# Attention with all four score tiles of a head pair in one group, small row jobs between V and Q in the bank of z, and one reciprocal and one value scaling per pair

## The chip, the cores and the metric

The kernel runs on one core of one Trainium2 chip. The core has TensorE (PE, matrix products into PSUM), VectorE (DVE), ScalarE (ACT), GpSimd (POOL), and SyncE (SP), which only issues transfers. PSUM is eight banks of 128 x 512 fp32 numbers. The metric is the device time of the whole program in microseconds (us).

## The reference

Four layers follow each other on x of 8 rows (batch entries) x 512 positions x 128 features: softmax attention with 16 heads, a mixture of experts, linear attention with an MLP, and the same mixture of experts again. The change touches the first layer, and one bank name in what follows it:

```python
def _L0_attn_a_ref(x, W_K, W_Q, W_V, W_O):      # 16 heads of 64
    k = jnp.einsum('ahe,bce->bach', W_K, x)
    q = jnp.einsum('ahe,bce->bach', W_Q, x)
    v = jnp.einsum('ahe,bce->bach', W_V, x)
    scores = jnp.einsum('bach,baCh->bacC', k, q)
    mask = jnp.tril(jnp.ones((seq, seq), dtype=scores.dtype))
    masked = jnp.tril(scores) - 10000000000.0 * (1.0 - mask)
    attn = jax.nn.softmax(masked / np.sqrt(d_head), axis=-1)
    z = jnp.einsum('bach,bacC->baCh', v, attn)
    z_flat = z.transpose(0, 2, 1, 3).reshape(b, seq, -1)
    return jnp.einsum('ef,bcf->bce', W_O, z_flat)
...
x = x + _L0_attn_a_ref(_layernorm(x, axis=-1), ...)
x = x + _L0_ffn_ref(_layernorm(x, axis=-1), ...)
```

The softmax runs over the axis C, up to the position c of the key side, so each of the 512 positions c has a row of scores of length c + 1. The sum over each row divides V, not the scores.

## The kernel before

**Tiling.** The order on every engine is written out by hand, and each engine runs its own list; semaphores tie them together. The attention stage goes over 8 rows b, in each over 8 head pairs g (`PAIRS`). The two heads of a pair lie in partitions 0 to 63 and 64 to 127. Positions c are cut into four tiles i of 128, and tile i has `width[i]` = 128, 256, 384, 512 columns of scores, since the mask cuts the rest. A pair was handled in two halves n = 2g and 2g + 1 (`HALVES`): the even half takes the "big" tile 3 and the "small" tile 0, the odd half takes tile 2 and tile 1.

**Work of a pair on TensorE.** `scores(b, n)` (L1159) makes the scores of a half: three products (high and low parts of K and Q) for each of the two heads. After the even half come V for a later pair (`project_V`, into `bankK`), Q for pair g + 1 (`project_Q`, into `bankQ`), the output product of an older pair (`out_of`, L1189, which needs the high and low part of its z), and K for pair g + 1 (`project_K`, into `bankK`). These projections all go through `matmul3` (L451 to L453). After the odd half comes `PV` (L1176) of the pair g - 1: probabilities times scaled V, summed over tiles in `bankZ`.

**The other engines.** VectorE adds the mask to each score tile and takes its negated maximum in one instruction (L1449, eight in a pair: four tiles x two heads), makes the low parts of Q, K and z (`low_Q` L1411, `low_K` L1416, `low_z` L1421), and inverts the sums of a half (`invert`, L1426). ScalarE takes the exponentials with their sums (L1350) and copies V, Q, K and z out of PSUM (L1329, L1318, L1322, L1335). GpSimd scales V by the inverted sums (`scale_V`, L1526), once in a half.

**Small row jobs.** Beside the pairs, each row b has jobs for its neighbours: the statistics, the norm and the transposes for the next row (`ahead`), the transposes that bring the output of the row before back (`turn_back`, L1199), and for the row before the router of the experts: transposes (L426), logits (L547), choice of two experts, ranks (L624 to L628), slots, and eight scatters from GpSimd (L675). Constants such as `TURN_AT = 5` name the half in which each stands. All TensorE jobs of this kind use `bankQ`, stand behind the `PV` of an odd half, and `project_Q` of the next pair waits for their readers. A semaphore tells how far each step is; `START` is its first value. `each_row` (L459) writes the eight rows one after another.

**After the rows**, the last pairs are finished, and `Folding` prepares weights of later layers; it uses banks 2 and 3 as `bankVO`.

## Time and profile before

| what | us |
|---|---|
| runs of the kernel, median (lowest to highest) of 3 | 1360.21 (1359.12 to 1361.42) |
| span of the profiled execution | 1361.0 |
| attention pairs, first score product to first score product of the last pair | 18.15 to 527.66 |
| PE busy in the span | 1219.8 (90%) |
| DVE, ACT, POOL busy in the span | 920.1, 824.2, 517.2 |

The page tells how long each engine was busy and where in the span. A busy engine need not be at its peak, so the step from the start of one instruction to the start of the next is what counts on TensorE. The profiled execution lies within the three runs, 0.8 us above their median. The views used further down are the busy time of each engine in a stretch, the timeline of one engine or of all (start, duration, what it is, and in brackets the idle time in front of it with what ended it), and the same busy time for VectorE alone.

### The profile page before, as it was taken

Reading aid. Unit: us, or ns where it says so; the run is one execution under the profiler, and the core shown is the slowest. Engines: PE = TensorE matmul, PEld = TensorE weight load, DVE = VectorE, ACT = ScalarE, POOL = GpSimd, SP = SyncE. Lnnn points to the kernel's source line nnn. Section 1 sums busy time; section 2 is a strip of 40 time slices with the busy share of each in tenths; the row PEclk is TensorE's granted clock in tenths of the full one; section 3 lists DMA queues with packets and bytes.
Section 4 is the critical chain, followed back from the end, with each engine's and each line's share of the span. In section 5 each row is a group of like instructions: output and inputs, shape, how many; then the busy total and the mean of one; then the engine's idle time right before and its main releaser. Section 6 shows DMA issues by size and latency. Waiting matters only on the chain. (4 is left out here: it accounts for less than half of the span.)

```text
span 1361.0 us, 27110 instructions
## 1 busy us (share of the span) xinstructions
PE 1219.8 (90%) x7787; PEld 924.5 (68%) x7787; DVE 920.1 (68%) x3602; ACT 824.2 (61%) x2478; POOL 517.2 (38%) x683
## 2 busy tenths in 40 slices
PE   6999999999999998599993999999996998199990
PEld 5666666666666665499982777777774665199890
DVE  6777888888888876444445788888874666244445
ACT  5888888888888886144441556555655675044440
POOL 2112332323333232545452343344433376545450
PEclk9999999999999999799996999999998999599995
DMA  9100000000000000222222000000000011222225
GB/s 295 42 1 1 9 9 9 10 9 10 9 10 9 10 13 5 68 63 70 70 67 66 17 17 16 17 1 1 1 1 1 15 40 36 73 64 71 68 71 193
DMA packets 54445, 52.92 MB, mean 39 GB/s; under 512 B 7341, under 2 KB 43098, under 8 KB 54330
## 3 DMA queue, kind: packets, MB, share of 16 engines
q1 hardware_dynamic: 36320, 29.39, 7.6%
q0 software_dynamic: 8928, 17.84, 3.9%
q10 hardware_dynamic: 9082, 4.33, 1.1%
q8 instruction: 52, 0.85, 0.3%
q14 instruction: 63, 0.52, 0.1%
HBM read 29.48 MB, written 22.05 MB: 38 GB/s over the span
## 5 line engine op out<-in xcount | busy, mean ns | idle before, releaser
L1350 ACT ACTIVATE prob<-prob,negmax 128x512 f32<-128x512 f32 (+3 forms) x512 | 283.0, 556 | 78.8 <-DVE negmax L1449 76.8
L1449 DVE CUSTOM_DVE_ANT_0 prob<-bank,mask 128x512 f32<-128x512 f32 (+3 forms) x512 | 227.7, 482 | 51.2 <-PE bank L1159 50.9
L1526 POOL TENSOR_TENSOR Vs<-Vh_sb,rinv 128x256 f32<-128x256 f32 x128 | 78.4, 612 | 364.6 <-DVE rinv L1426 364.4
L1047 POOL DMA_INDIRECT expert_out<-f_x_yb,f_x_to x142 | 136.5, 961 | 155.3 <-DVE f_x_yb L1035 100.5
L1176 PE MATMUL bank<-prob,Vs 128*64 128x512 f32 (+3 forms) x1024 | 151.9, 439 | 0.9 <-DVE zT_lo L1421 0.9
L675 POOL DMA_INDIRECT expert_in<-f_xn,f_slot x128 | 126.9, 991 | 51.2 <-issue 27.9
L979 PE MATMUL bank<-f_x_xbT,W_sb 128*128 128x256 f32 x568 | 138.5, 388 | 1.5 <-DVE f_x_xbT L1015 1.5
L1000 ACT ACTIVATE f_x_hid<-bank,cols 128x256 f32<-128x256 f32 x144 | 63.6, 475 | 93.0 <-PE bank L979 93.0
L979 PEld LDWEIGHTS bank<-f_x_xbT,W_sb 128*128 128x128 f32 x568 | 104.6, 194 | 14.7 <-DVE f_x_xbT L1015 2.9
L1176 PEld LDWEIGHTS bank<-prob,Vs 128*64 128x64 f32 x1024 | 63.4, 136 | 69.5 <-issue 59.4
L1000 ACT ACTIVATE prob<-bank,cols 128x256 f32<-128x256 f32 x140 | 61.1, 475 | 81.7 <-PE bank L979 81.7
L1032 DVE CAST f_x_to<-f_x_this_to 128x1 int32<-128x1 f32 x142 | 21.4, 151 | 115.0 <-DMA expert_out<-f_x_yb,f_x_to 114.4
L1350 ACT ACTIVATION_READ_ACCUMULATOR prob<-prob,negmax 128x1 f32 x512 | 97.3, 190 | 0.0
L1159 PE MATMUL bank<-Q_hi,K_hi 64*128 64x512 f32 (+3 forms) x512 | 93.3, 357 | 2.7 <-DVE K_lo L1416 2.1
L1809 ACT ACTIVATE yT_hi<-bank 128x512 fp32r<-128x512 f32 x64 | 38.3, 598 | 92.7 <-PE bank L1736 92.7
L1943 DVE SCALAR_TENSOR_TENSOR z_sb<-bank,ro,z_sb 128x128 f32<-128x128 f32 x256 | 88.5, 346 | 5.0 <-POOL ro L1877 1.5
L1159 PE MATMUL bank<-Q_lo,K_hi 64*128 64x512 f32 (+3 forms) x512 | 83.5, 318 | 0.0
L1159 PE MATMUL bank<-Q_hi,K_lo 64*128 64x512 f32 (+3 forms) x512 | 83.5, 318 | 0.0
L1159 PEld LDWEIGHTS bank<-Q_hi,K_hi 64*128 64x128 f32 x512 | 48.5, 183 | 44.4 <-issue 34.6
L1816 ACT ACTIVATE junk<-bank 128x128 f32<-128x128 f32 x256 | 68.7, 274 | 15.5 <-PE bank L453 3.4
L451 PE MATMUL bank<-WVO_hi,yT_hi 128*128 128x256 f32 x256 | 73.9, 289 | 2.4 <-DVE z_sb L1943 2.4
L453 PE MATMUL bank<-WVO_hi,yT_lo 128*128 128x256 f32 x256 | 71.5, 279 | 0.0
(263 smaller groups left out, 3183.6 us busy)
## 6 DMA issues: line engine op xcount, KB each, us to landing
f_x_xb<-expert_in SPq DMA_DIRECT2D x73, 130.0 KB
b_crows<-expert_out SPq DMA_DIRECT2D x16, 256.0 KB, 2.8
c_crows<-expert_out SPq DMA_DIRECT2D x16, 256.0 KB, 4.1
expert_out<-f_x_yb,f_x_to POOLq DMA_INDIRECT x142
expert_in<-fill ACTq DMA_DIRECT2D x16, 130.0 KB, 2.6
x_sb<-in_L_attn_a_x_dram SPq DMA_DIRECT2D x8, 256.0 KB, 6.2
W_sb<-in_L_ffn_W_dram SPq DMA_DIRECT2D x1, 2048.0 KB, 9.9
expert_in<-f_xn,f_slot POOLq DMA_INDIRECT x128
```

The source lines that it names most:

```text
L451: nc.tensor.matmul(ps, lhsT_hi, rhs_hi, start=True, stop=False)
L453: return nc.tensor.matmul(ps, lhsT_lo, rhs_hi, start=False, stop=stop)
L675: pool.indirect_dma_start(xg, bass.IndirectOffsetOnAxis(ap=self.slot[:, u, t, k:k + 1], axis=0), self.norm.xn_sb[:, u, t, :], None).then_i ...
L979: nc.tensor.matmul(self.bankH[c][:, 0:BLK], W1_sb[:, e, c * P:(c + 1) * P], self.xbT[:, :], start=True, stop=True).then_inc(self.up_done[c ...
L1000: nc.scalar.activation(self.hid[:, c, :], self.bankH[c][:, 0:BLK], ACT.Relu, bias=b1_col[:, e * FC + c:e * FC + c + 1]).then_inc(self.hid_ ...
L1047: pool.indirect_dma_start(yg, bass.IndirectOffsetOnAxis(ap=self.to[:, t:t + 1], axis=0), self.yb[:, t, :], None).then_inc(self.stored[t], 16)
L1159: mm = nc.tensor.matmul(bankS[which][a][:, 0:width[i]], left[r, g % 2, tile], right[r, g % 2, 0:width[i]], start=(right is Q_hi and left i ...
L1176: mm = nc.tensor.matmul(bankZ[heads, 0:width[tiles_of(m)[which]]], Vs[:, m % 4, AT[which], heads], prob[:, m % 4, a, columns_of(m, which)] ...
L1350: nc.scalar.activation(mine, mine, ACT.Exp, scale=-1.0, bias=negmax[:, n % 4, t, a:a + 1], accum_out=rowsum[:, n % 4, t, a:a + 1]).then_in ...
L1449: nc.vector.tensor_tensor_reduce(out=prob[:, n % 4, a, columns_of(n, which)], in0=bankS[which][a][:, 0:width[i]], in1=mask[:, T - width[i] ...
L1526: nc.gpsimd.tensor_tensor(Vs[:, m % 4, :, :].rearrange("p t (a d) -> p t a d", a=2), V_sb[:, quarter % 2, small:big + 1:big - small, pair] ...
L1943: nc.vector.scalar_tensor_tensor(out=tile, in0=bankO[s % 2 * 2 + m // 2][:, o:o + D], scalar=ro[:, s % 2, m:m + 1], in1=tile, op0=ALU.mult ...
```

## The change

1. **Scores.** `scores(b, g)` makes all four tiles of a pair in one group, in the order 1, 3, 0, 2. Tile 1 goes into `bankQ` and `bankK`, tile 3 into the big banks, tiles 2 and 0 share the small banks (tile 0 behind the columns of tile 2). One wait for the masks of the pair before stands ahead of the group; V waits until the two masks of tile 1 are done.
2. **Order on TensorE.** A pair is now: scores, V, small row job (`between`), Q, `out_of` of pair g - 2 (before: g - 3), K, `PV` of pair g - 1. `between` waits in each pair until `low_z` of pair g - 2 is done, whether a job follows or not. The jobs write `bankZ`; `between_read` makes `PV` wait for their readers.
3. **VectorE.** The eight masks of a pair stand in a row; behind the second comes the reciprocal of all eight sums of pair g - 1, behind the third `low_z`, behind the sixth the readers of a row job; then `low_Q`, `low_K`, and only then the other row work of the pair.
4. **ScalarE.** It begins a pair with z of pair g - 2, then eight exponentials, with V behind the third, Q behind the fourth and K behind the sixth.
5. **GpSimd.** One `scale_V` per pair over 512 numbers a partition in place of two over 256; up to two scatters stand together in a pair.
6. `prob`, `Vs`, `negmax`, `rowsum` and `rinv` are laid out in two buffers by pair in place of four by half; `Folding` uses banks 0 and 3.

```diff
-            ahead = Ahead("a", st, LN, x_sb, 1.0, None, split=True, whole=False, bankT=bankQ)
+            ahead = Ahead("a", st, LN, x_sb, 1.0, None, split=True, whole=False, bankT=bankZ)
...
-            TURN_AT = 5
-            AHEAD_STATS, AHEAD_RSTD, AHEAD_NORM, AHEAD_TR = 0, 1, 2, 3
-            X_ADD, ROUTE_STATS, ROUTE_RSTD, ROUTE_NORM, ROUTE_TR, ROUTE_LOGITS, ROUTE_RANK = 5, 6, 7, 8, 9, 11, 15
+            AHEAD_STATS, AHEAD_RSTD, AHEAD_NORM, AHEAD_TR = 0, 1, 1, 3
+            TURN_AT, ROUTE_STATS, ROUTE_RSTD, ROUTE_NORM, ROUTE_TR, ROUTE_LOGITS, ROUTE_RANK = 2, 2, 3, 3, 4, 5, 7
...
+            SCATTERS = {0: (0, 1), 1: (2,), 2: (3, 4), 3: (5,), 4: (6, 7)}
+
+            ORDER = [(i, a) for i in (1, 3, 0, 2) for a in range(2)]
...
+                    def scores(b, g):
+                        pe.wait_ge(masked, START + (b * PAIRS + g) * PER_PAIR)
+                        pe.wait_ge(q_ready, START + b * PAIRS + g + 1)
+                        pe.wait_ge(k_ready, START + b * PAIRS + g + 1)
+                        for i in (1, 3, 0, 2):
...
+                    def between(b, u, g, first, last):
...
+                        pe.wait_ge(zT_ready, START + b * PAIRS + g - 1)
+                        if g == TURN_AT and not first:
+                            turn_back(b - 1)
+                        if g == AHEAD_TR and not last:
+                            ahead.pe_transpose(pe, b + 1, 1 - u)
...
+                        for g in range(PAIRS):
+                            scores(b, g)
...
+                                pe.wait_ge(masked, START + (b * PAIRS + g) * PER_PAIR + 2)
                                 project_V(u if quarter < NT else 1 - u, quarter % NT, part)
...
+                            between(b, u, g, first, last)
+                            if ahead_too:
                                 project_Q(*here)
-                                if g >= 3:
-                                    out_of(b, g - 3)
+                            if g >= 2:
+                                out_of(b, g - 2)
...
                                 project_K(*here)
...
+                            between_read(b, g, first, last)
...
                             if g >= 1:
-                                PV(b, n - 3)
-                                PV(b, n - 2)
+                                PV(b, g - 1)
...
-                    invert(B - 1, HALVES - 1)
                     low_z(B - 1, PAIRS - 2)
+                    invert(B - 1, PAIRS - 1)
                     low_z(B - 1, PAIRS - 1)
```

**TensorE, second half of a pair, before** (a_xnT with WVO is K for the next pair, Q with K are scores, prob with Vs is `PV`; L1199 is the row job `turn_back`):

```order
L451 MATMUL bank<-a_xnT_hi,WVO_hi 128x512
L452 MATMUL bank<-a_xnT_lo,WVO_hi 128x512
L453 MATMUL bank<-a_xnT_hi,WVO_lo 128x512
L1159 MATMUL bank<-Q_hi,K_hi 128x384 x2
L1159 MATMUL bank<-Q_lo,K_hi 128x384 x2
L1159 MATMUL bank<-Q_hi,K_lo 128x384 x2
L1159 MATMUL bank<-Q_hi,K_hi 128x256 x2
L1159 MATMUL bank<-Q_lo,K_hi 128x256 x2
L1159 MATMUL bank<-Q_hi,K_lo 128x256 x2
L1176 MATMUL bank<-prob,Vs 64x512 x2
```

**TensorE, the same place of the changed program**, from K on:

```order
L454 MATMUL bank<-a_xnT_hi,WVO_hi 128x512
L455 MATMUL bank<-a_xnT_lo,WVO_hi 128x512
L456 MATMUL bank<-a_xnT_hi,WVO_lo 128x512
L1176 MATMUL bank<-prob,Vs 64x512 x2
L1176 MATMUL bank<-prob,Vs 64x128 x2
L1176 MATMUL bank<-prob,Vs 64x256 x2
L1176 MATMUL bank<-prob,Vs 64x384 x2
L1164 MATMUL bank<-Q_hi,K_hi 128x256 x2
L1164 MATMUL bank<-Q_lo,K_hi 128x256 x2
L1164 MATMUL bank<-Q_hi,K_lo 128x256 x2
L1164 MATMUL bank<-Q_hi,K_hi 128x512 x2
```

The score group between K and `PV` is gone; `PV` follows K at once, and the scores of all tiles follow `PV`.

**VectorE, before, around the choice of experts** (halves 12 and 13 of a row; ISA is the mask instruction with its accumulator read, f_ex to f_row_sel belong to the router):

```order
L593 CAST f_topidf<-f_topid 128x32
L594 TENSOR_TENSOR gates<-f_top,f_rrec 128x8
L1449 ISA prob,negmax<-bank,mask 128x384
...
L1426 RECIPROCAL rinv<-rowsum 128x4
L1416 TENSOR_TENSOR K_lo<-bank,K_hi 128x512
L1449 ISA prob,negmax<-bank,mask 128x256
...
L600 COPY f_xn<-token 128x4
L602 COPY f_xn<-f_topidf 128x4
L604 TENSOR_TENSOR f_is_k<-expert_id,f_topidf 128x32 x2
```

**VectorE, the same router work in the changed program**, at the end of pair 6 of a row:

```order
L1411 TENSOR_TENSOR Q_lo<-bank,Q_hi 128x512
L1416 TENSOR_TENSOR K_lo<-bank,K_hi 128x512
L582 TENSOR_REDUCE f_rsum<-f_ex 128x4
L584 MAX f_top<-f_ex 128x8 x4
L589 RECIPROCAL f_rrec<-f_rsum 128x4
L591 MAX_INDEX f_topid<-f_top,f_ex 128x8 x4
L596 CAST f_topidf<-f_topid 128x32
L597 TENSOR_TENSOR gates<-f_top,f_rrec 128x8
L603 COPY f_xn<-token 128x4
L605 COPY f_xn<-f_topidf 128x4
L607 TENSOR_TENSOR f_is_k<-expert_id,f_topidf 128x32 x2
```

Masks of score tiles stood between the two parts of this work; now both parts stand together, behind `K_lo`.

## Rows read from the trace of the kernel before

**Rows 1.** Busy time of each engine in a stretch of the pairs (start:end, length):

```profile
core 0: us, PE busy (x) PEld busy (x) DVE busy (x) ACT busy (x) POOL busy (x), PEclk, DMA share, GB/s
215.00:275.00 60.00, 59.31 (x430) 40.48 (x430) 49.15 (x209) 50.58 (x154) 20.14 (x30) 1.00 0.03 11
```

**Rows 2.** Timeline of PE over one pair: start, duration, engine, line, operation:

```profile
283.86 0.50 PE L1159 MATMUL bank<-Q_hi,K_hi 64*128 64x512 f32 x2
...
285.05 0.39 PE L451 MATMUL bank<-WVO_hi,a_xnT_hi 128*128 128x256 f32 x1
...
285.87 0.40 PE L451 MATMUL bank<-a_xnT_hi,A_hi 128*128 128x512 f32 x1
...
288.04 0.44 PE L1159 MATMUL bank<-Q_hi,K_hi 64*128 64x384 f32 x2
...
289.12 2.37 PE L1176 MATMUL bank<-prob,Vs 128*64 128x512 f32 x16
...
291.43 0.66 PE L426 MATMUL bank<-ident,a_xn 128*128 128x128 f32 x4
...
292.01 0.51 PE L1159 MATMUL bank<-Q_hi,K_hi 64*128 64x512 f32 x2
```

**Rows 3.** Timeline of PE at row jobs; brackets: idle before, and its releaser:

```profile
276.09 0.19 PE L624 MATMUL bank<-f_sel,before_bf 128*128 128x32 bf16 x1
...
296.06 0.50 PE L451 MATMUL bank<-a_xnT_hi,WVO_hi 128*128 128x512 f32 x1 [0.21 <-ACT Vh_sb L1329]
...
319.24 0.50 PE L451 MATMUL bank<-a_xnT_hi,A_hi 128*128 128x512 f32 x1 [0.39 <-ACT f_xnT L433]
...
324.90 1.06 PE L547 MATMUL bank<-Wr_sb,f_xnT 128*128 128x8 f32 x8
325.89 0.50 PE L1159 MATMUL bank<-Q_hi,K_hi 64*128 64x512 f32 x2
...
341.13 0.19 PE L624 MATMUL bank<-f_sel,before_bf 128*128 128x32 bf16 x1
```

**Rows 4.** Timeline of DVE in the same pair:

```profile
285.02 0.69 DVE L1449 CUSTOM_DVE_ANT_0 prob<-bank,mask 128x512 f32<-128x512 f32 x1 [0.74 <-PE bank L1159]
...
285.64 0.69 DVE L1449 CUSTOM_DVE_ANT_0 prob<-bank,mask 128x512 f32<-128x512 f32 x1
...
286.74 0.69 DVE L1421 TENSOR_TENSOR zT_lo<-bank,zT_hi 128x512 fp32r<-128x512 f32 x1
...
290.16 0.17 DVE L1426 RECIPROCAL rinv<-rowsum 128x4 f32<-128x4 f32 x1
290.25 0.66 DVE L1416 TENSOR_TENSOR K_lo<-bank,K_hi 128x512 fp32r<-128x512 f32 x1
...
290.83 0.41 DVE L1449 CUSTOM_DVE_ANT_0 prob<-bank,mask 128x256 f32<-128x256 f32 x1
```

**Rows 5.** Timeline of ACT in the same pair:

```profile
286.48 0.58 ACT L1329 ACTIVATE Vh_sb<-bank 128x512 f32<-128x512 f32 x1
...
286.96 0.59 ACT L1318 ACTIVATE Q_hi<-bank 128x512 fp32r<-128x512 f32 x1
...
287.44 0.72 ACT L1350 ACTIVATE prob<-prob,negmax 128x512 f32<-128x512 f32 x1
...
288.14 0.40 ACT L1350 ACTIVATE prob<-prob,negmax 128x128 f32<-128x128 f32 x1
```

**Rows 6.** DVE busy in four stretches: router norm, experts' choice (two parts), statistics:

```profile
312.82:314.87 2.05, 2.05 (x9) 1.00 0.19 65
330.20:331.60 1.40, 1.33 (x17) 1.00 0.00 0
333.91:334.76 0.85, 0.78 (x8) 1.00 0.00 0
345.66:346.96 1.30, 1.16 (x9) 1.00 0.15 51
```

**Rows 7.** Timeline of all engines behind the last pair's scores:

```profile
527.66 0.50 PE L1159 MATMUL bank<-Q_hi,K_hi 64*128 64x512 f32 x2
...
535.03 0.66 DVE L1421 TENSOR_TENSOR zT_lo<-bank,zT_hi 128x512 fp32r<-128x512 f32 x1
535.25 0.61 POOL L1526 TENSOR_TENSOR Vs<-Vh_sb,rinv 128x256 f32<-128x256 f32 x1 [2.06 <-DVE rinv L1426]
535.74 0.20 PEld L1176 LDWEIGHTS bank<-prob,Vs 128*64 128x64 f32 x4 [1.37 <-DVE zT_lo L1421]
```

More of the change, by code:

```diff
@@ new lines, in between_read @@
+                    def between_read(b, g, first, last):
+                        if g == TURN_AT and not first:
+                            pe.wait_ge(x_done, START + b)
+                        if g == AHEAD_TR and not last:
+                            pe.wait_ge(xnT_ready, START + b + 2)
+                            pe.wait_ge(ahead.lo_ready, START + b + 2)
+                        if g == ROUTE_TR and not first:
+                            pe.wait_ge(route.xnT_ready, START + b)
+                        if g == ROUTE_LOGITS and not first:
+                            pe.wait_ge(route.step, START + (b - 1) * route.DVE_STEPS + route.LOGIT)
+                        if g == ROUTE_RANK and not first:
+                            pe.wait_ge(route.step, START + (b - 1) * route.DVE_STEPS + route.PLACE)
@@ L1207, in row @@
                     def row(b, u):
                         first, last = is_row(b, 0), is_row(b, B - 1)
-                        for n in range(HALVES):
-                            g = n // 2
-                            scores(b, n)
-                            if n % 2 == 0:
-                                if g == PAIRS - 1 and last:
-                                    out_of(b, g - 3)
-                                    continue
+                        for g in range(PAIRS):
+                            scores(b, g)
+                            ahead_too = g < PAIRS - 1 or not last
+                            here = (b, u, g + 1) if g < PAIRS - 1 else (b + 1, 1 - u, 0)
+                            if ahead_too:
@@ L1222, in row @@
-                                if n == AHEAD_TR + 1 and not last:
-                                    pe.wait_ge(xnT_ready, START + b + 2)
-                                    pe.wait_ge(ahead.lo_ready, START + b + 2)
-                                if n == ROUTE_TR + 1 and not first:
-                                    pe.wait_ge(route.xnT_ready, START + b)
-                                if n == ROUTE_LOGITS + 1 and not first:
-                                    pe.wait_ge(route.step, START + (b - 1) * route.DVE_STEPS + route.LOGIT)
@@ L1257, in row @@
-                            if n == ROUTE_RANK and not first:
-                                pe.wait_ge(q_ready, START + b * PAIRS + g + (1 if last else 2))
-                                route.pe_rank(pe, b - 1, 1 - u)
+                                PV(b - 1, PAIRS - 1)
                     pe.wait_ge(startup.const, startup.CONSTS)
@@ L1375, in row @@
+                            if g == TURN_AT - 1 and not first:
+                                evac_out(b - 1)
+                            if g == ROUTE_LOGITS and not first:
                                 route.act_exp(act, b - 1, 1 - u)
@@ new lines, in row @@
+                                if j == 2 and g >= 2:
+                                    low_z(b, g - 2)
+                                elif j == 2 and not first:
+                                    low_z(b - 1, PAIRS + g - 2)
+                                if j == 5:
+                                    if g == 0 and first:
+                                        startup.dve_cols(dve)
+                                        folding.dve_early(dve)
+                                    if g == TURN_AT and not first:
+                                        x_add(b - 1)
+                                    if g == AHEAD_TR and not last:
+                                        ahead.dve_low(dve, b + 1, 1 - u, xnT_ready)
+                                    if g in (ROUTE_LOGITS, ROUTE_RANK) and not first:
+                                        ROUTE_DVE[g][0](dve, b - 1, 1 - u)
@@ L1472, in row @@
+                            if g < PAIRS - 1 or not last:
+                                low_Q(*here)
+                                low_K(*here)
                             if not last:
-                                if n == AHEAD_STATS:
+                                if g == AHEAD_STATS:
                                     if first:
```

318 lines of the change are left out of this document (138 added, 180 removed).

## The prediction

> **What bounds the kernel now.** I read the busy times by stretch first. In a stretch in the middle of the pairs TensorE is busy 59.31 of 60.00 us at full clock (1.00 of 2.4 GHz), VectorE 49.15, ScalarE 50.58, GpSimd 20.14 [rows 1]. So TensorE sets the pace, and only what shortens its list, or the waits in it, brings time. Then I read TensorE's timeline as steps from start to start. A pair without a row job takes 283.86 to 291.43, 7.57 us: first score group 1.19, V 0.82, Q with `out_of` and K 2.17, second score group 1.08, `PV` 2.31 [rows 2]. A row of eight pairs takes 341.13 - 276.09 = 65.04 [rows 3], while 8 x 7.57 = 60.56. The other 4.5 us of a row are row jobs and the waits they cause: 0.58 for four transposes [rows 2], 0.99 for the logits, and waits such as 0.39 for the router's copy and 0.21 for V's [rows 3]. A product that starts after a wait or a change of tile shape lasts 0.50 in place of 0.40, so a fresh start costs 0.10 [rows 2, 3].
>
> **One score group in place of two.** The products are the same. Two groups cost 1.19 + 1.08; one group saves a fresh start (0.10) and one change of shape at its end (0.09, taken like the start: the rows don't separate it, its bounds are 0 and 0.2). It costs 2.08. TensorE alone would need 2.08 + 0.82 + 2.17 + 2.31 = 7.38 for a pair.
>
> **The new wait between V and Q.** `between` waits in every pair for `low_z`. What stands ahead of it on VectorE: the first mask, which began 1.16 behind the first score product for 512 columns [rows 2, 4]. Tile 1 has 256 columns; its three products are shorter by about 0.12 each, so the mask can begin at 0.80. Two masks of 256 columns take 0.34 each (0.41 less the 0.07 by which neighbours overlap), the reciprocal 0.09 (290.16 to 290.25), a mask of 512 columns 0.62, `low_z` 0.69 [rows 4]. That ends at 0.80 + 0.68 + 0.09 + 0.62 + 0.69 = 2.88. TensorE followed `low_z` by 0.05 where it waited for it (535.69 to 535.74) [rows 7]: Q can start at 2.93. V ends at 2.08 + 0.82 = 2.90. The two are level, and Q then pays a fresh start. A pair is 2.93 + 0.10 + 2.17 + 2.31 = 7.51, only 0.06 under 7.57. The gain of the merged group is thus nearly eaten by the wait. Queued behind this wait are Q, `out_of`, K and `PV`, and whoever needs them; every us by which VectorE comes late to its first mask is a us of TensorE.
>
> **Row jobs between V and Q.** A job now stands where TensorE starts afresh anyhow, so it costs its time less 0.10: three times transposes 0.48, logits 0.89, ranks about 0.12 (bounds 0.05 and 0.25). Sum 2.45. Their readers have Q, `out_of` and K as cover, 2.17, and the readers (a copy of 0.6 to 0.8 and a subtraction of 0.7) fit. The old waits of 0.39, 0.21 and the like go.
>
> **What is late next: VectorE's row work.** It stands behind `K_lo` now, in fewer and larger pieces. When is `K_lo` done? ScalarE begins the third exponential at 1.57 + 0.74 = 2.31; 0.70 for it, V's copy from 3.09 when V is there, 0.48; the fourth exponential 0.70 to 4.27; Q's copy 0.48; two of 128 columns 0.39 each; K's copy begins at 5.53 and lasts 0.58 [rows 5]; `K_lo` takes 0.58 more [rows 4] and ends at 6.7. The next pair wants VectorE at 7.51 + 0.80 = 8.31, so 1.6 us are free. Statistics (1.30) fit, the norm of the next row (half of the 2.05 of the router's norm) fits. The router's norm (2.05) does not: in pair 3 the copy of the transposes pushes `K_lo` to 7.27, it ends at 9.32, and pair 4, which is 7.98 behind, wants VectorE at 8.78: 0.54 late. The experts' choice (1.40 + 0.85) ends at 8.97 against 8.31: about 0.7 late [rows 6]. Together 1.24 in a row of eight pairs.
>
> **GpSimd, reciprocal, scatters.** One scaling of 512 in place of two of 256 lasts between 0.61 and 1.22 [rows 7]; I take 1.1. It starts near 1.9 of a pair, `PV` needs it at 5.1, so even with two scatters behind it nobody waits. The saved reciprocal is 0.09 of VectorE in the second half of a pair, where it is waiting for K: nothing. In the Trainium skill, GPSIMD Engine Reference, section 3.1, a two-input elementwise operation costs about 2.6 cycles per element, an estimate of 0.55 us for the 256 more, thus 1.16; no run here shows it yet. The sum below would be 0.06 higher by it, at the tail alone.
>
> **Tail.** Before, the last `PV` began 8.08 behind the first score product of the last pair [rows 7]. Now: VectorE 0.7 late, ranks at 3.6, their reader done at 4.7, `PV` of pair 6 from 4.8 to 7.2, its copy to 7.8, `low_z` to 8.5. The last reciprocal stands behind that, 8.6, scaling to 9.85, last `PV` at 9.9: 1.8 later. I take 1.9.
>
> **The sum.** A full row: 8 x 7.51 + 2.45 + 1.24 = 63.77, which is 1.27 less than 65.04; six such rows give 7.6. Rows 0 and 7 have fewer jobs; I take 2.3 for both, with half a us from the start, where the first K no longer waits behind statistics. Minus the tail: 7.6 + 2.3 - 1.9 = 8.0. Against the profiled span, 1361.0 - 8.0 = 1353.0. The median is 0.8 below that span, so 1352.2.
>
> **Rivals.**
> *TensorE keeps its own pace.* If the wait at Q is not felt, a pair is 7.38. It gives 0.13 more in the six pairs of a row that are not late, 6 us in all: 1346. For it: 2.88 and 2.90 are level. Against it: the wait has to be over 0.1 earlier for the fresh start to vanish too.
> *The chain is a tenth longer.* The first mask at 0.90 in place of 0.80 (a shape that no row shows) gives 0.8 a row, 6.4 in all: 1359, no change.
> *Slower: `K_lo` comes late.* VectorE's row work can't start before it, and ScalarE is 84% busy [rows 1]. If ScalarE delivers K so late that `K_lo` ends just when the next scores start (0.8 later than above), the two late pairs cost 0.8 more each, both statistics 0.5 each and the next row's norm 0.2: 2.8 a row, 19 over seven rows, and the time is 1364. It decides from about 0.43 later on, where it costs 1.14 a row and eats the gain. For it: three copies in one pair (V, Q, K) and row jobs on ScalarE shift K; against: I count 1.6 us of slack.
> *GpSimd blocks VectorE.* The scaling, now twice as long, lies beside the mask and `low_z` of the chain. If it held `low_z` from 2.2 to 3.0, each of 64 pairs would lose 0.8, 51 in all: 1403. Against it: `low_z` and masks beside scalings last the same 0.69 as elsewhere [rows 4, 7]. The Trainium skill, SBUF — State Buffer, section "Who interferes with whom", says that only VectorE instructions with two SBUF inputs or in a two-port mode contend with GpSimd; mask and `low_z` read one input from PSUM, so by that rule, too, this rival falls.
> *The change does less than it says.* Merged reciprocal and scaling are off the path; they give nothing in any case above.
>
> **How the numbers follow.** Chances: the forecast 0.48 (1347 to 1356, from the bounds of the shape change, the ranks and the two late pairs), TensorE's pace 0.12, longer chain 0.20, late `K_lo` 0.18, GpSimd 0.02. The range that leaves out no more than 0.2 reaches from 1344 to 1365. A measurement of this kernel can tell 0.2% (2.7 us) from no change. Faster by more than that: 0.48 + 0.12 = 0.60; within it: 0.20; slower: 0.20.
>
> **What would show it.** In the timeline after: Q starts 2.9 to 3.1 behind the first score product in pairs without a job, with a duration of 0.50; a pair takes 7.5; pairs 4 and 7 show V or Q waiting 0.5 to 0.7 for VectorE; waits of TensorE for the copies of row jobs are gone; the last `PV` is about 10 behind the last pair's first score product. It is wrong if the first masks begin later than 0.9, if `K_lo` ends later than 7.2 of a pair, or if more than two pairs of a row are late.

## The result, and the profile after

| | kernel before | changed kernel |
|---|---|---|
| median of 4 runs (lowest to highest), us | 1360.07 (1359.12 to 1361.42) | 1351.72 (1348.61 to 1353.20) |
| ratio (95% interval) | 1 | 0.9937 (0.9925 to 0.9949) |
| span of the profiled execution | 1361.0 | 1346.7 |
| first score product of the last pair | 527.66 | 516.40 |
| last `PV` | 535.74 | 526.46 |
| behind it | 825.3 | 820.2 |

The change saves 8.4 us in the medians, which ends 0.5 us below the forecast of 1352.2. A second series of the same two kernels, further down, gave a ratio of 0.9948, or 5.9 us, so that the forecast came this close to the median is partly luck.

The profiled execution is the shortest of the four; its span is 14.3 us below that of before. A time is 1.9 us longer than the span of the same execution (1348.61 against 1346.7), so the profile of the kernel before, with its span of 1361.0, stands for a time near 1362.9: 2.8 above the median of that kernel and not, as the section on the profile before says, within its runs. The two profiles thus lie further apart than the medians. 9.3 of the 14.3 us lie in the attention, up to the last `PV`. The rest lies behind it, in code that the change hardly touches (one bank name); an experiment below takes that up.

Busy time in the same 60 us as in [rows 1] (columns as there):

```profile
215.00:275.00 60.00, 58.94 (x431) 40.46 (x429) 50.12 (x209) 52.19 (x156) 19.74 (x23) 1.00 0.03 9
```

TensorE has a little more idle time than before (1.06 us against 0.69) and yet a row is 1.2 us shorter. The table of pairs below tells where: an ordinary pair gives 0.05, 0.4 in a row, and the pairs with row jobs, which cost 4.5 us a row more than ordinary ones before, now cost 3.6 more. So most of the gain comes in the pairs with row jobs, whose place is new, and less in the ordinary ones. An ordinary pair, TensorE's timeline; it answers to [rows 2]:

```profile
333.75 0.39 PE L1164 MATMUL bank<-Q_hi,K_hi 64*128 64x256 f32 x2
...
335.86 0.39 PE L454 MATMUL bank<-WVO_hi,a_xnT_hi 128*128 128x256 f32 x1
...
336.67 0.50 PE L454 MATMUL bank<-a_xnT_hi,A_hi 128*128 128x512 f32 x1
337.01 0.40 PE L455 MATMUL bank<-a_xnT_lo,A_hi 128*128 128x512 f32 x1
...
338.96 2.37 PE L1176 MATMUL bank<-prob,Vs 128*64 128x512 f32 x16
...
341.27 0.39 PE L1164 MATMUL bank<-Q_hi,K_hi 64*128 64x256 f32 x2
```

Scores 2.11, V 0.81, Q at 2.92 with its first product 0.50 long in place of 0.40, the pair 7.52. VectorE in the same pair, as [rows 4]:

```profile
334.55 0.42 DVE L1448 CUSTOM_DVE_ANT_0 prob<-bank,mask 128x256 f32<-128x256 f32 x1 [1.02 <-PE bank L1164]
...
335.25 0.20 DVE L1426 RECIPROCAL rinv<-rowsum 128x8 f32<-128x8 f32 x1
335.36 0.64 DVE L1448 CUSTOM_DVE_ANT_0 prob<-bank,mask 128x512 f32<-128x512 f32 x1
...
335.93 0.69 DVE L1421 TENSOR_TENSOR zT_lo<-bank,zT_hi 128x512 fp32r<-128x512 f32 x1
...
339.94 0.69 DVE L1416 TENSOR_TENSOR K_lo<-bank,K_hi 128x512 fp32r<-128x512 f32 x1 [0.56 <-ACT K_hi L1323]
```

The first mask begins 0.80 behind the first score product, `low_z` ends at 335.93 + 0.69 = 336.62, and Q starts 0.05 later. The late pairs are there too. In pair 4 the router's norm ends on VectorE just where the next mask starts, 1.44 behind the scores' start of 364.59 and not 0.80, and TensorE waits at the row job:

```profile
363.98 1.10 DVE L404 TENSOR_SCALAR f_xn<-x_sb,f_mv,f_power 128x128 f32<-128x128 f32 x4
365.00 1.11 DVE L410 TENSOR_SCALAR x_sb<-x_sb,f_power 128x128 f32<-128x128 f32 x4
366.03 0.42 DVE L1448 CUSTOM_DVE_ANT_0 prob<-bank,mask 128x256 f32<-128x256 f32 x1
```

```profile
368.14 0.65 PE L427 MATMUL bank<-ident,f_xn 128*128 128x128 f32 x4 [0.32 <-DVE zT_lo L1421]
```

And pair 7 of a row (scores from 325.28), where the first mask comes 1.62 behind, after the experts' choice:

```profile
326.74 0.21 DVE L619 TENSOR_REDUCE f_row_sel<-f_sel 128x8 f32<-128x32 bf16 x1
326.90 0.42 DVE L1448 CUSTOM_DVE_ANT_0 prob<-bank,mask 128x256 f32<-128x256 f32 x1
```

```profile
327.73 0.38 PE L454 MATMUL bank<-WVO_hi,a_xnT_hi 128*128 128x256 f32 x1 [0.28 <-DVE negmax L1448]
...
329.02 0.19 PE L627 MATMUL bank<-f_sel,before_bf 128*128 128x32 bf16 x1 [0.32 <-DVE zT_lo L1421]
```

The tail, which answers to [rows 7]:

```profile
516.40 0.39 PE L1164 MATMUL bank<-Q_hi,K_hi 64*128 64x256 f32 x2
...
521.28 2.37 PE L1176 MATMUL bank<-prob,Vs 128*64 128x512 f32 x16
525.08 0.50 PE L1186 MATMUL bank<-zT_hi,WOT_hi 128*128 128x512 f32 x1 [1.42 <-DVE zT_lo L1421]
...
526.46 2.38 PE L1176 MATMUL bank<-prob,Vs 128*64 128x512 f32 x16 [0.42 <-POOL Vs L1524]
```

In the tables below "row" is the time from the scores of one pair to the same pair of the next row, a mean of five rows (63.88 in the changed kernel, 65.04 before), and a pair's step goes from the start of its scores to that of the next, the median of rows 1 to 6, which all have the same jobs:

| pair | 0 | 1 | 2 | 3 | 4 | 5 | 6 | 7 |
|---|---|---|---|---|---|---|---|---|
| kernel before, us | 7.55 | 8.15 | 8.91 | 7.57 | 8.21 | 9.19 | 7.57 | 7.89 |
| changed kernel, us | 7.52 | 7.51 | 7.92 | 7.91 | 8.52 | 8.41 | 7.52 | 8.46 |
| its row job | none | none | turn back | transposes | router's transposes | logits | none | ranks |

The medians of the changed kernel add up to 63.77, 0.1 less than the row. The rest stands in single pairs that are longer in both of its profiles, at the same places: pair 7 of row 5 takes 8.80, pair 2 of row 3 takes 8.14. The last section comes back to them.

### The profile page after: what moved, and what is told of

It reads as the page before. It is cut to its first block and busy times, and to the rows that moved or that the text cites. A ratio compares the mean times of both kernels' runs of the same rounds, so it can differ in the third digit from the quotient of the medians.

```text
span 1346.7 us, 26854 instructions
## 1 busy us (share of the span) xinstructions
PE 1208.7 (90%) x7787; PEld 917.0 (68%) x7787; DVE 912.4 (68%) x3538; ACT 829.2 (62%) x2478; POOL 505.1 (38%) x619
## 5 line engine op out<-in xcount | busy, mean ns | idle before, releaser
L1354 ACT ACTIVATE prob<-prob,negmax 128x256 f32<-128x256 f32 (+3 forms) x512 | 283.2, 556 | 47.6 <-DVE negmax L1448 47.5
L1448 DVE CUSTOM_DVE_ANT_0 prob<-bank,mask 128x256 f32<-128x256 f32 (+3 forms) x512 | 223.9, 480 | 41.9 <-PE bank L1164 41.6
L1524 POOL TENSOR_TENSOR Vs<-Vh_sb,rinv 128x512 f32<-128x512 f32 x64 | 66.6, 1041 | 365.7 <-DVE rinv L1426 365.7
L1164 PE MATMUL bank<-Q_hi,K_hi 64*128 64x256 f32 (+3 forms) x512 | 89.2, 344 | 2.3 <-DVE K_lo L1416 2.3
L1164 PE MATMUL bank<-Q_lo,K_hi 64*128 64x256 f32 (+3 forms) x512 | 82.9, 319 | 0.0
L1164 PE MATMUL bank<-Q_hi,K_lo 64*128 64x256 f32 (+3 forms) x512 | 82.2, 317 | 0.0
```

The source lines that it names most:

```text
L1164: mm = nc.tensor.matmul(score_bank(i, a), left[r, g % 2, tile], right[r, g % 2, 0:width[i]], start=(right is Q_hi and left is K_hi), stop= ...
L1354: nc.scalar.activation(mine, mine, ACT.Exp, scale=-1.0, bias=negmax[:, g % 2, i, a:a + 1], accum_out=rowsum[:, g % 2, i, a:a + 1]).then_in ...
L1448: nc.vector.tensor_tensor_reduce(out=prob[:, g % 2, a, columns(i)], in0=score_bank(i, a), in1=mask[:, T - width[i]:], scale=-1.0, scalar=H ...
```

## The experiments

Twelve kernels ran, each against the kernel before on the same chip. There were three chips, on which the kernel before took 1361.6, 1360.9 and 1358.9 us, so the ratios are to be compared rather than the medians. All but `changed_again`, `four_edits` and `five_edits` change one thing in the changed kernel, whose own ratios are 0.9937 and, in a second series, 0.9948. One timed ratio has an interval of 0.12 to 0.25% to each side, so small effects are read from the row's length in the trace, which repeats to 0.02 us between the two profiles of the changed kernel. The others have one profile each.

| kernel | median, us | ratio (interval) | row, us | row against 63.88 |
|---|---|---|---|---|
| choice_split | 1347.3 | 0.9885 (0.9861 to 0.9908) | 63.08 | -0.80 |
| norm_split | 1350.0 | 0.9909 (0.9884 to 0.9933) | 63.26 | -0.62 |
| wait_with_a_job_only | 1352.0 | 0.9921 (0.9896 to 0.9945) | 63.62 | -0.26 |
| job_behind_Q | 1353.1 | 0.9938 (0.9912 to 0.9963) | 63.72 | -0.16 |
| reciprocal_behind_low_z | 1349.0 | 0.9913 (0.9895 to 0.9930) | 63.48 | -0.40 |
| two_reciprocals | 1355.5 | 0.9953 (0.9932 to 0.9973) | 64.26 | +0.38 |
| two_scalings | 1352.2 | 0.9939 (0.9920 to 0.9957) | 63.90 | +0.02 |
| two_score_groups | 1398.3 | 1.0278 (1.0260 to 1.0295) | 69.08 | +5.20 |
| tail_reciprocal_first | 1353.1 | 0.9944 (0.9921 to 0.9967) | 63.88 | 0 |
| changed_again | 1353.1 | 0.9948 (0.9932 to 0.9965) | 63.90 | +0.02 |
| four_edits | 1337.1 | 0.9830 (0.9812 to 0.9847) | 62.04 | -1.84 |
| five_edits | 1335.0 | 0.9820 (0.9803 to 0.9836) | 61.58 | -2.30 |

### The group itself: two_score_groups

```diff
-                    def scores(b, g):
+                    def scores(b, g, tiles=(1, 3)):
...
-                        for i in (1, 3, 0, 2):
+                        for i in tiles:
...
+                            scores(b, g, (0, 2))
                             between(b, u, g, first, last)
```

> The changed kernel, with the score tiles of a pair in two groups again: tiles 1 and 3 ahead of V, tiles 0 and 2 behind it, ahead of the wait between V and Q. Theory (one group saves a fresh start and a change of shape): the two groups take together 0.1 to 0.2 us more than 2.08 to 2.10; V comes at 1.25 and must wait until the second mask is read, near 1.5, so it loses 0.25 more; the wait for low_z is covered, Q at 0.70 to 0.80. A pair goes from 7.50 to 7.80 to 7.95, 20 to 28 us in all, 1372 to 1380. Rival (grouping itself is worth nothing, and VectorE's chain was the bound): the pair stays within 0.1 of 7.50.

TensorE in a pair without a row job:

```profile
346.54 0.38 PE L1164 MATMUL bank<-Q_hi,K_hi 64*128 64x256 f32 x2
...
348.19 0.39 PE L454 MATMUL bank<-WVO_hi,a_xnT_hi 128*128 128x256 f32 x1 [0.33 <-DVE negmax L1449]
...
349.08 0.33 PE L1164 MATMUL bank<-Q_hi,K_hi 64*128 64x128 f32 x2
...
350.13 0.49 PE L454 MATMUL bank<-a_xnT_hi,A_hi 128*128 128x512 f32 x1
```

The first group with V's wait is 1.65, so 1.32 without it; the second 1.05. Together 2.37, which is 0.26 more than one group, against an expected 0.1 to 0.2. The wait is 0.33 in place of 0.25, V is 0.08 longer. A pair takes 8.18, 0.66 more; I expected 0.3 to 0.45, and 1372 to 1380 us, where 1398.3 was measured. The sign was right and the sizes were too small. The rival (grouping is worth nothing) falls. But not all of the 0.66 is the worth of the group: half of it is V's wait for the masks of tile 1, which only this way of splitting brings. In the kernel before, whose two groups had no such wait, they took 1.19 + 1.08 = 2.27, so against that kernel the one group of 2.11 saves 0.16.

### The chain to Q: two_reciprocals, reciprocal_behind_low_z

```diff
-                        nc.vector.reciprocal(rinv[:, g % 2, :, :], rowsum[:, g % 2, :, :]).then_inc(rinv_ready, 1)
+                        nc.vector.reciprocal(rinv[:, g % 2, 0:2, :], rowsum[:, g % 2, 0:2, :])
+                        nc.vector.reciprocal(rinv[:, g % 2, 2:4, :], rowsum[:, g % 2, 2:4, :]).then_inc(rinv_ready, 1)
```

> The changed kernel, with the reciprocal done as two of four columns each, as before the change, both ahead of low_z. Theory (the chain of masks, reciprocal and low_z sets when Q starts): 0.09 to 0.12 us more in every pair that waits for low_z, 62 of 64, so 6 to 7 us more, 1358. Rival (the chain has slack against V's end): 0 to 1 us, 1352. It also prices the reciprocal that the change saves, which I had put at nothing.

```diff
-                                if j == 1 and g >= 1:
-                                    invert(b, g - 1)
...
                                 if j == 2 and g >= 2:
                                     low_z(b, g - 2)
...
+                                if j == 2 and g >= 1:
+                                    invert(b, g - 1)
...
```

> The changed kernel, with the one reciprocal of a pair behind low_z in place of ahead of it: VectorE's chain ahead of TensorE's wait between V and Q is 0.09 to 0.12 us shorter. Theory (V's end and the chain are level, and what the wait costs is the fresh start): in ordinary pairs the chain now ends about 0.05 ahead of V. If a wait that is already met costs nothing, Q goes from 0.80 to 0.70 and an ordinary pair from 7.50 to 7.40, 2 to 3 us in all, and the two late pairs shrink by 0.1 as well, together 3 to 4 us, 1348. Rival (the wait in the list costs the fresh start even when it is met): 0.1 in the late pairs alone, 1 to 1.5 us, 1350.5.

With two reciprocals, `low_z` begins 2.24 behind the scores' start of 344.84 and not 2.18, and it comes out at TensorE: from V to Q 0.88 in place of 0.81, a row 0.38 longer, 2.7 us in seven rows. The theory holds in kind and the rival (slack) falls; I expected 0.09 to 0.12 in each of 62 pairs, 6 to 7 us, but two short reciprocals cost the chain only 0.06 more than one.

```profile
346.35 0.17 DVE L1426 RECIPROCAL rinv<-rowsum 128x4 f32<-128x4 f32 x1
346.43 0.15 DVE L1427 RECIPROCAL rinv<-rowsum 128x4 f32<-128x4 f32 x1
...
347.08 0.69 DVE L1421 TENSOR_TENSOR zT_lo<-bank,zT_hi 128x512 fp32r<-128x512 f32 x1
```

With the reciprocal behind `low_z` the chain is ahead of V:

```profile
341.75 0.69 DVE L1421 TENSOR_TENSOR zT_lo<-bank,zT_hi 128x512 fp32r<-128x512 f32 x1
...
342.54 0.46 PE L454 MATMUL bank<-a_xnT_hi,A_hi 128*128 128x512 f32 x1
```

`low_z` ends at 342.44, Q starts at 342.54 and lasts 0.46: neither the 0.40 of a product in a series nor the 0.50 of a fresh start. The ordinary pairs are 7.46, a row 0.40 shorter, 2.8 us in seven rows. That is near the time the theory gave, but neither mechanism hit: a wait met 0.1 ahead still costs about 0.06. Without it, in the next experiment, the start is free.

### The wait without a job: wait_with_a_job_only

```diff
-                        pe.wait_ge(zT_ready, START + b * PAIRS + g - 1)
+                        if (g == AHEAD_TR and not last) or (g in (TURN_AT, ROUTE_TR, ROUTE_LOGITS, ROUTE_RANK) and not first):
+                            pe.wait_ge(zT_ready, START + b * PAIRS + g - 1)
```

> The changed kernel, where TensorE waits between V and Q for low_z only in the pairs that have a row job there; in the others only the product behind Q waits for it. Theory (in an ordinary pair this wait and the fresh start behind it cost 0.12 us): the three pairs of a row without a job go from 7.50 to 7.38, 0.36 in a row, 2.5 to 3 us in all, 1349. Rival (the wait costs nothing, the pair's 7.50 is the products' own time): 0, 1351.7, and Q keeps a duration of 0.80.

```profile
341.33 0.39 PE L454 MATMUL bank<-a_xnT_hi,A_hi 128*128 128x512 f32 x1
341.56 0.40 PE L455 MATMUL bank<-a_xnT_lo,A_hi 128*128 128x512 f32 x1
...
342.03 0.39 PE L1186 MATMUL bank<-zT_hi,WOT_hi 128*128 128x512 f32 x1
```

Q's first product is back at 0.39, and pairs 0, 1 and 6 take 7.39 each. That is the 0.12 of the theory, and TensorE's own pace of 7.38. The output product at 342.03 now waits for the same `low_z`, which ended at 341.30, and also lasts 0.39: a wait that was met 0.7 ahead costs nothing. A row gains only 0.26 of 0.36, because pair 6 now ends earlier while the experts' choice on VectorE doesn't: pair 7 is 8.58 in place of 8.46. In the time (1352.0) the 1.8 us can't be told from nothing; the trace decides here.

### The late pairs: choice_split, norm_split

In `choice_split` `dve_rmax` and `dve_shift` go behind the logits in the middle of pair 5 and ScalarE's `act_exp` behind its K copy, so that half of the choice can stand behind pair 5:

```diff
+            LATE_DVE = {5: (route.dve_top, route.dve_topid),
+                        6: (route.dve_ids, route.dve_is_k, route.dve_sel, route.dve_row_sel),
+                        7: (route.dve_picked, route.dve_slotf, route.dve_slots)}
```

> The changed kernel, with the experts' choice spread over three places of VectorE's list: maximum and shift of the logits stand behind the logits in the middle of pair 5, sums, maxima and their indices behind K_lo of pair 5, only the rest (about 1.1 us) behind K_lo of pair 6. Theory (pair 7 is late because this work ends after the next pair's scores are there): the late pair shrinks by nearly all of its 0.82 us, 0.6 to 0.8 in each of seven rows, so 4 to 5.5 us less than the changed kernel (1351.7), about 1347. Rival (TensorE's late pair has another cause, or the wait only moves to pair 6): within 1 us of the changed kernel, and pair 7 or pair 6 still takes 0.5 us more than an ordinary one.

In `norm_split` `dve_normalise` is called in two parts, the update of x (L410) in the middle of pair 4:

```diff
+                                    if g == ROUTE_NORM + 1 and not first:
+                                        route.norm.dve_normalise(dve, b - 1, 1 - u, "y")
...
-                                    route.dve_normalise(dve, b - 1, 1 - u)
+                                    dve.wait_ge(route.scattered[1 - u], route.landed(b - 1, 1 - u))
+                                    route.norm.dve_normalise(dve, b - 1, 1 - u, "xn")
```

> The changed kernel, with the router's norm cut in two on VectorE: the four that make its input stay behind K_lo of pair 3, the four that update x in place go to the middle of pair 4, where VectorE waits 0.76 and 0.56 us for ScalarE. Theory (pair 4 is late because the norm's 2.05 us end after the scores are there): the 0.6 us by which pair 4 is late go, in seven rows about 4 us, to 1347.5. Rival (the mask chain of pair 4 is then late itself, since 1.02 us are put ahead of Q_lo): the lateness comes back in pair 5, and the time stays at 1351 to 1352.

The first masks tell it at once. With the choice split, that of pair 7 begins 0.81 behind the scores' start in six of seven rows, in place of 1.63; the pair takes 7.65 in place of 8.46, and its neighbours stay as they were. With the norm split, the mask of pair 4 waits for the scores again and not for the norm, and pair 4 takes 7.92 in place of 8.52 in five of six rows (8.17 in row 1, though its mask is in time there too; the cause was not followed):

```profile
362.69 1.11 DVE L405 TENSOR_SCALAR f_xn<-x_sb,f_mv,f_power 128x128 f32<-128x128 f32 x4
...
364.10 0.42 DVE L1449 CUSTOM_DVE_ANT_0 prob<-bank,mask 128x256 f32<-128x256 f32 x1 [0.30 <-PE bank L1165]
...
367.10 1.11 DVE L411 TENSOR_SCALAR x_sb<-x_sb,f_power 128x128 f32<-128x128 f32 x4
```

Pair 5 stays at 8.40: the 1.03 us now ahead of `low_Q` fill VectorE's idle time. Both theories hold. Rows gain 0.80 and 0.62 (0.73 for the first if its last row, with one mask 0.35 late in pair 6, is counted in), 5.6 and 4.3 us in seven; the ratios (7.1 and 3.8 us below the changed kernel's 0.9937) agree within their intervals.

### The place of the job: job_behind_Q

```diff
-                            between(b, u, g, first, last)
+                            if g == 0 and first:
+                                between(b, u, g, first, last)
                             if ahead_too:
                                 project_Q(*here)
+                            if not (g == 0 and first):
+                                between(b, u, g, first, last)
...
```

> The changed kernel, with the row job and its wait for low_z behind Q in place of ahead of it (and ScalarE's copy for it behind Q's copy). Q's 0.80 us then cover the chain of masks and low_z. Theory: ordinary pairs 7.38 in place of 7.50 (0.36 in a row); in the late pairs 4 and 7 the 0.46 us that TensorE waits behind V go (0.9 in a row); a job now breaks up products and costs its whole 0.58 or 0.99 in place of 0.41 or 0.91, 0.05 to 0.1 more for each pair that has one (0.4 in a row). In sum 0.8 to 1.0 in a row, 6 to 8 us less, 1344 to 1346. Rival (the job's readers come too late, since only the product of z and K are left as their cover): PV waits up to 0.5 us in four pairs of a row, and the time is 1352 or more.

Pairs 0, 1, 6 are at 7.39 as expected, 2 and 5 gain 0.08 and 0.13, 7 gains 0.32. But pair 3 rises from 7.91 to 8.51 and pair 4 from 8.52 to 8.73. VectorE, ScalarE and TensorE in pair 3:

```profile
360.17 0.60 ACT L438 ACTIVATE a_xnT_hi<-bank 128x512 fp32r<-128x512 f32 x1
```

```profile
360.80 0.69 DVE L449 TENSOR_TENSOR a_xnT_lo<-bank,a_xnT_hi 128x512 fp32r<-128x512 f32 x1 [1.52 <-ACT a_xnT_hi L438]
```

```profile
361.59 2.37 PE L1176 MATMUL bank<-prob,Vs 128*64 128x512 f32 x16 [0.61 <-issue]
```

The copy of the transposes stands behind Q's on ScalarE and ends at 360.77, its subtraction at 361.49, and `PV` starts only then, 0.7 late; the page calls that wait "issue", its size and place show what it is. The rival (readers too late) took the two pairs whose readers are a copy and a subtraction, the theory the others. In sum -0.16 in a row, where 0.8 to 1.0 was expected, and no measurable change of time (1353.1 for an expected 1344 to 1346). Which jobs may move behind Q is what it taught: turn-back, logits and ranks.

### Off the path: two_scalings, tail_reciprocal_first

```diff
-                        nc.gpsimd.tensor_tensor(
-                            Vs[:, g % 2, :, :].rearrange("p t (a d) -> p t a d", a=2),
...
+                        for t in range(0, NT, 2):
+                            ins = nc.gpsimd.tensor_tensor(
+                                Vs[:, g % 2, t:t + 2, :].rearrange("p t (a d) -> p t a d", a=2),
...
```

> The changed kernel, with GpSimd's scaling of V done as two of 256 columns in place of one of 512. Theory (the scaling begins near 2 us of a pair and PV needs it at 5, so it is off the path): two times 0.61 in place of 1.04, done 0.2 later, and nothing in the time, 1351 to 1352; the last PV 0.1 to 0.2 later. Rival (GpSimd's time beside VectorE's work holds VectorE up): masks and low_z change their duration, and the time moves by over 3 us.

```diff
+                    invert(B - 1, PAIRS - 1)
                     low_z(B - 1, PAIRS - 2)
-                    invert(B - 1, PAIRS - 1)
                     low_z(B - 1, PAIRS - 1)
```

> The changed kernel, with the last pair's reciprocal ahead of the two last low_z on VectorE, behind the last row only. Theory (the last PV waits for GpSimd's scaling, which waits for this reciprocal, which stands behind a low_z of 0.6 us that waits for the PV before): the 0.42 us that the last PV waits for the scaling go, and the last PV begins 9.6 in place of 10.06 us behind the last pair's first score product; in the whole time 0.4 us, which the timed runs can't tell from nothing. Rival (out_of's wait for low_z is what comes last there): 0 in the trace as well.

Costliest GpSimd group of the value scaling, in the changed kernel and with two scalings (instructions, busy us, mean ns, idle before):

```profile
L1524 POOL TENSOR_TENSOR Vs<-Vh_sb,rinv 128x512 f32<-128x512 f32 x64 | 66.6, 1041 | 365.7 <-DVE rinv L1426 365.7
```

```profile
L1525 POOL TENSOR_TENSOR Vs<-Vh_sb,rinv 128x256 f32<-128x256 f32 x128 | 75.6, 610 | 355.9 <-DVE rinv L1426 355.9
```

Two scalings take 1.18 us a pair (75.6 / 64) for 1.04, and the row stays at 63.90. VectorE's masks and `low_z` keep their durations beside either (0.66 and 0.69). The merged scaling brings nothing, as forecast, and doesn't harm VectorE. With the last reciprocal first, the last `PV` begins 9.57 behind the last pair's scores in place of 10.06, and its wait for GpSimd is gone; in the whole time it doesn't show.

The tail has a second source of differences. In `norm_split`, `wait_with_a_job_only` and `job_behind_Q` the last `PV` begins 11.55, 11.80 and 11.69 behind the last pair's scores, 1.5 to 1.7 later than in the changed kernel, which is as much as seven rows of the last two gain. TensorE's clock had fallen there. 4 to 8 us behind the last pair's scores, of the changed kernel and of `norm_split`, with the granted clock behind the brackets (0.57 in the mean means a part at 1.2 and not 2.4 GHz):

```profile
520.40:524.40 4.00, 3.21 (x21) 1.34 (x19) 2.55 (x18) 3.38 (x11) 0.00 (x0) 1.00 0.00 0
```

```profile
517.36:521.36 4.00, 4.00 (x19) 1.86 (x19) 2.48 (x17) 2.78 (x10) 0.00 (x0) 0.57 0.00 0
```

In both TensorE had waited about as long for `low_z` just before, 1.57 and 1.58 us. So the same wait was followed by a fall of the clock in one execution and by none in the other. Each kernel has one profile, so whether its edit or chance decides was not tested.

### What the profile of one execution is worth: changed_again

> The changed kernel once more, beside the others on the same chip. Theory (the profiled execution was 5 us below the median of the timed ones because the unedited code behind the attention took less in it, by chance): its pace inside the attention is the same to 0.1 us in a row (63.9), its ratio to the kernel before 0.993 to 0.995, and the part behind the attention is longer than in the first profile by 2 to 6 us. Rival (the change itself gains 5 us behind the attention): the part behind it is again as short as in the first profile, within 1 us.

The row is 63.90. Behind the last `PV` there are 824.6 us, 4.4 more than in the first profile of the same kernel. In the profiles of all kernels of this study that part lies between 822.5 and 825.9, and 825.3 before the change; 820.2 is the one outlier. So the change does not act there. What made it short in that execution stays open; the difference between the two profiles is not in one place, but is 1.7 us at 250 us behind the last `PV`, 3.8 at 575 and 4.5 near the end. A second difference is at the start, in busy time and granted clock (the number behind the brackets) from 28 to 32 us, of before, of the changed kernel, and of its second profile:

```profile
28.00:32.00 4.00, 4.00 (x19) 2.62 (x19) 2.98 (x14) 3.48 (x11) 0.61 (x1) 0.63 1.04 336
```

```profile
28.00:32.00 4.00, 3.87 (x24) 2.34 (x26) 3.00 (x13) 4.00 (x14) 2.16 (x3) 1.00 1.06 328
```

```profile
28.00:32.00 4.00, 4.00 (x20) 2.51 (x18) 2.18 (x11) 2.73 (x8) 1.77 (x3) 0.80 1.03 322
```

TensorE had waited more than 2 us for the first K's low part just ahead of this stretch, before and after the change. From the first score product of the program to that of pair 3 the changed kernel took 22.2 us in its first profile and 23.6 in its second: 1.4 us go with the clock there. The theory holds in the row and in the part behind the attention; the ratio, 0.9948, is within what it gave.

### All together: four_edits, five_edits

`four_edits` joins choice_split, norm_split, wait_with_a_job_only and tail_reciprocal_first. `five_edits` (six, with the tail) adds reciprocal_behind_low_z and moves three kinds of job behind Q:

```diff
+                            behind_Q = g in (TURN_AT, ROUTE_LOGITS, ROUTE_RANK)
+                            if not behind_Q:
+                                between(b, u, g, first, last)
                             if ahead_too:
                                 project_Q(*here)
+                            if behind_Q:
+                                between(b, u, g, first, last)
```

> The changed kernel with choice split, norm split, wait for low_z only with a job, and last reciprocal first; all jobs stay ahead of Q and the reciprocal ahead of low_z. Added up from the single runs: 0.80 + 0.62 + 0.26 in a row, 1.7 in seven rows, 12 us: 1339 to 1341, a row at 62.0 to 62.2. Rival (the late pairs hand the same wait to one another): a row stays over 62.8. The difference from the kernel with all edits, about 4 us, is what the place behind Q and the reciprocal bring once nothing else is late.

> The changed kernel with all that helped: choice split over three places, norm split, wait for low_z only with a job, turn-back, logits and ranks behind Q (the two transposes, whose readers need more cover, stay ahead of Q), reciprocal behind low_z, last reciprocal first. If the gains are separate they add up: pairs 0, 1, 6 at 7.40, pair 2 at 7.83, 3 at 7.77, 4 at 7.83, 5 at 8.28, 7 at 7.55, a row 61.5 in place of 63.9, 2.4 in a row, 17 us with the tail: 1334 to 1337. Rival (once TensorE is faster, ScalarE's and VectorE's chain to K_lo bounds, since ScalarE is 84% busy): the pairs stay at 7.6 or more and the time at 1342 or more.

| pair | 0 | 1 | 2 | 3 | 4 | 5 | 6 | 7 |
|---|---|---|---|---|---|---|---|---|
| four_edits, us | 7.39 | 7.38 | 7.92 | 7.90 | 7.92 | 8.40 | 7.39 | 7.62 |
| five_edits, us | 7.39 | 7.39 | 7.84 | 7.85 | 7.85 | 8.28 | 7.39 | 7.60 |

A row of 61.58 for 61.5 expected, 1335.0 us for 1334 to 1337. The gains add up; the three edits bring 1.68 to a row singly and 1.84 in `four_edits`. More than the sum came, since pair 7 no longer gives back 0.12 for an earlier pair 6; `four_edits` took 1337.1 us, less than the 1339 to 1341 expected. The difference of the two kernels in time is 2.1 us, where I expected 4; by their rows it is 0.46, 3.2 us in seven. The stretch of [rows 1] in `five_edits`:

```profile
215.00:275.00 60.00, 60.00 (x460) 41.19 (x459) 51.70 (x215) 53.12 (x162) 18.34 (x21) 1.00 0.03 10
```

TensorE has no idle time left in it. What remains in this stage is TensorE's own list. This version is 1.8% faster than the kernel before and, by 1335.0 against 1353.1 on the same chip, 1.3% faster than the changed one.

## Why the prediction was right, step by step

| step of the prediction | forecast | measured |
|---|---|---|
| one score group | 2.08 | 2.11 |
| TensorE alone, a pair | 7.38 | 7.39 without the wait |
| first mask behind the first score product | 0.80 | 0.80 |
| Q behind the first score product, its duration | 2.93, 0.50 | 2.92, 0.50 |
| ordinary pair | 7.51 | 7.52 |
| jobs: transposes, logits, ranks | 0.48, 0.89, 0.12 | 0.40, 0.89, 0.13 |
| sum of jobs in a row | 2.45 | 2.22 |
| late pair 4, late pair 7 | 0.54, 0.7 | 0.60, 0.81 |
| end of `K_lo` in an ordinary pair | 6.7 | 6.9 |
| row | 63.77 | 63.88 (medians of its pairs: 63.77) |
| rows 1 to 6 | -7.6 | -7.1 |
| rows 0 and 7 | -2.3 | -4.2 |
| tail | +1.9 | +2.0 |
| attention in all | -8.0 | -9.3 |

**The middle of the rows** went as worked out. The two errors in it cancel, which is luck: jobs were cheaper (0.08 for each group of transposes), the lateness dearer (0.06 and 0.1). The lateness is what the two splits took away, 8.52 less 7.92 and 8.46 less 7.65, and the job what then stays above 7.52. No run puts the row jobs back behind `PV` by themselves, so that their new place brings most of the row's gain is read from the table of pairs and not tested. That the group's gain is nearly eaten by the wait is shown from both sides: taking the wait away brings 0.12 in an ordinary pair, lengthening its chain costs.

**The late pairs** were the step most worth making. VectorE's row work, whole behind `K_lo`, makes pairs 4 and 7 late, and each is cured by splitting that work (with the choice, ScalarE's exponential moves too).

**One term was mis-sized: rows 0 and 7.** I took 2.3 for both. Row 0 gained 2.8 and row 7 gained 1.4. From the first score product to that of pair 3 the kernel before takes 25.1 us and the changed one 22.2. A part of that is the clock at 28 to 32 us, which was 0.63 in the one and 1.00 in the other, and is no gain of the change: with 0.80 the changed kernel takes 23.6, a gain of 1.5, and since 0.80 is still above 0.63, a part of the 1.5 may be clock as well. In that second profile the last `PV` came at 527.48, 8.3 us before that of the kernel before, in place of 9.3. I had seen one cause of the rest, the K behind the statistics, and put it at 0.5; no run parts it further.

**The reciprocal** I had costed at nothing, with the saved one in idle time. That was half of it. The one that is left moved into the chain ahead of Q, where I counted its 0.09, and keeping two there costs 0.38 in a row.

**The step from span to time** was sound only by its result. I took 0.8 off a span of 1353.0, but a time is 1.9 us longer than its span, and the profile of before lay 2.8 above the median. What remains is the median of before less the gain, 1360.2 - 8.0 = 1352.2.

**The rivals.** TensorE's own pace did not come, the wait costs 0.12 in a pair. The longer chain did not come, the first mask is at 0.80. The late `K_lo` did not come: in an ordinary pair it ends at 6.9, earlier than the 7.2 that I had named as the bound. In pairs with a row job it ends at 7.0 to 8.2, but those pairs are longer too, and no more than two of a row, 4 and 7, find VectorE late. GpSimd beside VectorE did nothing: mask and `low_z` take 0.66 and 0.69 us beside one scaling of 1.04 us and beside two of 0.61. By the Trainium skill, SBUF — State Buffer, section "Who interferes with whom", a VectorE instruction with at most one SBUF input, outside the two-port modes, does not contend with GpSimd; mask and `low_z` read one input from PSUM, and the trace agrees. The Trainium skill, GPSIMD Engine Reference, section 3.1, led to an estimate of 1.16 us for the scaling of 512; the trace has 1.04, so the second 256 columns cost 0.43 and not 0.55.

## What to carry to other kernels

Read one pair of the loop as a chain from the first product to the wait that a change adds, and put it beside what the bounding engine does until then: here 2.88 against 2.90, and a fresh start, told the pair's length to 0.01 us. Next, list the side work of each helper engine behind the last step that the next round needs, and compare its end with that round's first demand; work that ends later than that belongs in two places. A job may move behind a product only as far as its slowest reader, a copy and then a subtraction, still ends ahead of the next writer of the bank.

## What the runs showed of the hardware that I had not expected

- A wait that was met 0.1 us ahead still lengthens TensorE's next product: 0.46 us, against 0.50 where it waits in earnest and 0.39 in a series without a wait. A wait that was met 0.7 us ahead costs nothing (0.39).
- TensorE's granted clock was between 0.61 and 0.80 in the mean at 28 to 32 us (part of the time at 1.2 and not 2.4 GHz), behind waits of over 2 us for the first K, in 5 of the 14 profiles, and was 1.00 in the other 9. The changed kernel had it once so and once so; it moves the time by over 1 us. In the tail the clock fell within 4 to 8 us of the last pair's scores in 3 of the 13 profiles of kernels with the new order (0.57 to 0.71 in the mean), behind waits of 1.58 to 1.73 us; `two_reciprocals` had one of 1.67 at that place and kept 1.00. There it costs 1.5 to 1.7 us.
- VectorE's first mask comes 0.35 us later than in the other rows in pair 7 of row 5, in 12 of the 13 profiles with the new order (1.98 behind the scores in place of 1.63 in the changed kernel, 1.16 in place of 0.81 in `choice_split`, `four_edits` and `five_edits`), and in those last three also in pair 6 of row 6. The one exception is `two_reciprocals`, which has more instructions on VectorE; there it is pair 0 of row 7 (1.17). So it belongs to a place in the program and not to chance. The page names only TensorE as its releaser, which was no later than elsewhere; the cause wasn't tested. In the changed kernel, where VectorE's work before it ends at 390.51 + 0.21 = 390.72:

```profile
391.02 0.42 DVE L1448 CUSTOM_DVE_ANT_0 prob<-bank,mask 128x256 f32<-128x256 f32 x1 [0.31 <-PE bank L1164]
```
